# GpSimd takes the sine product of the rotary embedding, VectorE the cosine product out of PSUM

## The reference, cut to what matters

```python
q = l2norm(q) * qs
k = l2norm(k) * ksc
...
q = q * cos * scale + rotate_half(q) * sin * scale
k = k * cos / scale + rotate_half(k) * sin / scale
```

## Time and profile before

| | us |
|---|---|
| median of 3 runs | 1446.84 |
| lowest, highest | 1443.94, 1450.88 |
| the profiled execution | 1459.8 |
| its span, first to last instruction | 1458.1 |

### The profile page before, as it was taken

How to read it: one execution, slowest core, us unless ns; L and a number is a source line. 1 busy time by engine, 2 the same in 40 slices (tenths; PEclk the granted TensorE clock), 3 DMA queues, 4 the chain that set the end, 5 groups by cost and what they waited for, 6 DMA issues and landing times. The chain is left out here.

```text
span 1458.1 us, 23509 instructions
## 1 busy us (share of the span) xinstructions
PE 1124.0 (77%) x8682; PEld 620.1 (43%) x8754; DVE 878.6 (60%) x1738; ACT 768.9 (53%) x1928; POOL 291.5 (20%) x228
## 2 busy tenths in 40 slices
PE   5986788678698668867869877886787976797677
PEld 4752453154374245325437425432534732542353
DVE  5549655963445865596345596468545467648744
ACT  1355674485235556447523556653942453945574
POOL 1105112410101411241010141033202033204210
PEclk9698899889859879988986988997997796999799
DMA  6003101400101310140010131023001014003100
GB/s 260 1 29 117 27 1 58 112 2 15 31 1 45 101 27 1 58 112 2 15 32 1 51 98 23 1 73 98 2 15 32 1 59 111 2 1 123 48 16 15
DMA packets 39201, 66.22 MB, mean 45 GB/s; under 512 B 5408, under 2 KB 19232, under 8 KB 37152
## 3 DMA queue, kind: packets, MB, share of 16 engines
q1 hardware_dynamic: 37920, 62.43, 14.0%
q10 hardware_dynamic: 1152, 2.10, 0.4%
HBM read 13.12 MB, written 2.10 MB: 10 GB/s over the span
## 5 line engine op out<-in xcount | busy, mean ns | idle before, releaser
L494 POOL TENSOR_TENSOR qk<-pc,ps_ 128x512 f32<-128x512 f32 x128 | 194.3, 1518 | 583.8 <-DVE ps_ L1040 583.8
L872 ACT ACTIVATE prob<-bank,negb,inv_norm 128x128 f32<-128x128 f32 x512 | 233.0, 580 | 57.3 <-DVE negb L1087 57.3
L1040 DVE TENSOR_TENSOR ps_<-rot,tab_s 128x512 f32<-128x512 f32 x128 | 172.5, 1347 | 25.9 <-DMA rot<-raw 25.9
L872 ACT ACTIVATION_READ_ACCUMULATOR prob<-bank,negb,inv_norm 128x1 f32 x512 | 163.3, 328 | 0.0
L510 PE MATMUL bank<-hTz,wb_s 128*128 128x512 f32 x256 | 139.5, 675 | 4.3 <-ACT sq L980 4.3
L1085 DVE TENSOR_REDUCE negb<-bank 128x8 f32<-128x1024 f32 x64 | 78.3, 1223 | 94.5 <-PE bank L628 94.4
L976 ACT ACTIVATE raw<-bank,vec_s 128x512 f32<-128x512 f32 x128 | 90.0, 703 | 81.6 <-PE bank L510 46.5
L500 POOL TENSOR_TENSOR prob<-prob,recb 128x512 f32<-128x512 f32 x64 | 66.7, 1041 | 320.1 <-DVE recb L1107 320.1
L1038 DVE TENSOR_TENSOR pc<-raw,tab_s 128x512 f32<-128x512 f32 x128 | 109.3, 854 | 18.2 <-ACT raw L976 18.1
L656 PE MATMUL bank<-probT,vS 128*64 128x64 f32 x1024 | 67.9, 231 | 38.6 <-issue 34.2
L510 PE MATMUL bank<-hTz,w_s 128*128 128x512 f32 (+1 forms) x192 | 87.8, 602 | 12.2 <-DVE hTz L1127 12.2
(11 more groups left out here) (151 smaller groups left out, 2020.8 us busy)
## 6 DMA issues: line engine op xcount, KB each, us to landing
rot<-raw SPq DMA_DIRECT2D x256, 128.0 KB, 2.0
vS<-vB SPq DMA_DIRECT2D x24, 512.0 KB, 4.4
vS<-vB SPq DMA_DIRECT2D x8, 384.0 KB, 5.7
xn_tok<-x SPq DMA_DIRECT2D x5, 512.0 KB, 3.6
tab_s<-tabs SPq DMA_DIRECT2D x1, 2048.0 KB, 21.0
vS<-x SPq DMA_DIRECT2D x4, 512.0 KB, 3.7
out<-vS SPq DMA_DIRECT2D x8, 256.0 KB, 2.4
wb_s<-wb SPq DMA_DIRECT2D x1, 1536.0 KB, 16.6
```

The lines of the kernel that those rows point to most:

```text
L494: pool.tensor_tensor(dst, pc[:, j % 2, :], ps_[:, j % 2, :], ALU.add).then_inc(sum_rdy, 1)
L872: ins = act.activation(prob[:, t % 2, g, h, :], s_bank[t % 2][:, g, h * P:(h + 1) * P], ACT.Exp, bias=negb[:, t % 2, g, h:h + 1], scale=qu ...
L1040: dve.tensor_tensor(ps_[:, j % 2, :], rot[:, jb % 4, :], st, ALU.mult).then_inc(prod_rdy, 1)
```

## The change

Keys: VectorE reads the product in PSUM, times scale vector and cosine, into `pc`, and that frees the bank. GpSimd makes the sine product into `ps_` (`exchanged`) and the sum. Queries: VectorE writes the cosine product back over the bank. GpSimd makes only the sine product, and VectorE adds bank and `ps_` into `qk` (`rotated`), which frees the bank. GpSimd runs one sine product ahead of its sums. ScalarE's square no longer frees the bank but raises `squared`.

With it: `prob` lies over `sq` rather than over `raw` and `rot`; the sums of squares of chunk 1 are handled in two parts, keys (`norms(1)`) and queries (`norms(2)`, within the second tile of the window attention); the shifted values go tile by tile, each with a semaphore of its own, those of chunk 0 behind the exchanges of the key tiles of chunk 1, those of chunk 1 at its end.

```diff
-        v_shifted = sem("values_shifted")
+        v_shifted = [sem(f"values_shifted{t}") for t in range(TILES)]
...
+        squared = sem("squares_ready")
+        turned_rdy = sem("query_cosine_products")
...
+        def key_sums(l, c, k):
+
+            return 4 + (l * CHUNKS + c) * 4 + k
...
-                        if jb % B_QK == B_QK - 1:
-                            c = jb // B_QK % CHUNKS
-                            for t in range(c * TPC, (c + 1) * TPC):
+                        if jb // B_QK % CHUNKS:
+                            k = jb % B_QK
+                            for t in range(TPC, TILES) if k == B_QK - 1 else (k,) if k < TPC else ():
                                 taken(sp, values_use(l, t))
-                            if l:
-                                sp.wait_ge(win_heads, on(l, 0))
-                            t0, t1 = c * TPC, (c + 1) * TPC
-                            sp.dma_start(vS[64:128, t0:t1, :], vB[0:64, t0:t1, :]).then_inc(v_shifted, 16)
-                            u1 = min(t1, TILES - 1)
-                            sp.dma_start(vS[0:64, t0 + 1:u1 + 1, :], vB[64:128, t0:u1, :]).then_inc(v_shifted, 16)
+                                if t == TPC:
+                                    sp.wait_ge(sums_turned, 3 * l + 3)
+                                if l:
+                                    sp.wait_ge(win_heads, on(l, 0))
+                                sp.dma_start(vS[64:128, t, :], vB[0:64, t, :]).then_inc(v_shifted[t], 16)
+                                if t + 1 < TILES:
+                                    sp.dma_start(vS[0:64, t + 1, :], vB[64:128, t, :]).then_inc(v_shifted[t + 1], 16)
...
+                    def exchanged(l, c, k):
+
+                        j = pair(l, c, k)
+                        jb = j - 4
+                        pool.wait_ge(rot_rdy[jb % 4], 32 * (jb // 4 + 1))
+                        if 2 <= k < 6:
+                            pool.wait_ge(sum_rdy, key_sums(l, c, k - 2) + 1)
+                        elif jb >= 2:
+                            l0, c0, k0 = (jb - 2) // 16, (jb - 2) // 8 % 2, (jb - 2) % 8
+                            taken(pool, qk_use(l0, c0, k0))
+                        else:
+                            pool.wait_ge(sum_rdy, 4)
+                        pool.tensor_tensor(ps_[:, j % 2, :], rot[:, jb % 4, :],
+                                           tab_s[:, 3 if k < 4 else 1, cc(c)], ALU.mult).then_inc(prod_rdy, 1)
...
+                                    exchanged(br, 0, 0)
+                                if k + 1 < B_QK or c + 1 < CHUNKS:
+                                    exchanged(br, c + (k + 1) // B_QK, (k + 1) % B_QK)
+                                if k >= 4:
+                                    continue
+                                pool.wait_ge(prod_rdy, j - 4 + 1)
+                                taken(pool, qk_use(br, c, k))
+                                pool.tensor_tensor(qk[:, qk_tile(k), cc(c)], pc[:, j % 2, :], ps_[:, j % 2, :],
                                                    ALU.add).then_inc(sum_rdy, 1)
...
+                        if t % TPC == 0:
+                            for k in range(4):
+                                taken(pe, qk_use(l, t // TPC, 4 + k))
...
-                                taken(pe, qk_use(l, c, k))
-                                mm = pe.matmul(bank[32 * m:32 * m + 32, 4 + c, :], sum_s[:, part, :], sq[:, m, :],
-                                               start=(part == 0), stop=(part == 1), skip_group_check=True)
+                                pe.wait_ge(squared, pair(l, c, k) - 3)
+                                alone = c == 1
+                                mm = pe.matmul(bank[32 * m:32 * m + 32, 4 + (c and not part), :], sum_s[:, part, :],
+                                               sq[:, m, :], start=(alone or part == 0), stop=(alone or part == 1),
+                                               skip_group_check=True)
...
-                                if tt == 0:
+                                if c == 0 and tt == 0:
                                     sum_squares(c, 1)
-                                if tt == 1:
-                                    turn_sums(c)
+                                if c == 0 and tt == 1:
+                                    turn_sums(0)
+                                if c and tt == 0:
+                                    turn_sums(1)
+                                if c and tt == 1:
+                                    sum_squares(c, 1)
+                        turn_sums(2)
...
-                                    act.wait_ge(prod_rdy, jb - 3)
+                                    act.wait_ge(rot_rdy[jb % 4], 32 * (jb // 4))
...
-                                act.activation(sq[:, jb % 4, :], bank[:, i % RING, :], ACT.Square)\
-                                   .then_inc(drained[i % RING], 1)
+                                act.activation(sq[:, jb % 4, :], bank[:, i % RING, :], ACT.Square).then_inc(squared, 1)
...
+                            if c:
+                                copy_sums(1)
...
+                        elif not A and k < 4:
+                            back = (key_sums(br, c, k - 2) if k >= 2 else key_sums(br, c - 1, k + 2) if c else
+                                    key_sums(br - 1, 1, k + 2) if br else 2 + k)
+                            dve.wait_ge(sum_rdy, back + 1)
...
-                            jb = j - 4
-                            dve.wait_ge(raw_rdy, RAW0[br] + c * 8 + k + 1)
-                            dve.tensor_tensor(pc[:, j % 2, :], raw[:, jb % 4, :], ct, ALU.mult)
-                            dve.wait_ge(rot_rdy[jb % 4], 32 * (jb // 4 + 1))
-                            dve.tensor_tensor(ps_[:, j % 2, :], rot[:, jb % 4, :], st, ALU.mult).then_inc(prod_rdy, 1)
+                            qs = V_L + br * VL_N + VL_QS + qk_tile(k) // 4
+                            dve.wait_ge(squared, j - 3)
+                            if k >= 4:
+                                dve.scalar_tensor_tensor(bank[:, i % RING, :], bank[:, i % RING, :], vec_s[:, qs:qs + 1], ct,
+                                                         ALU.mult, ALU.mult).then_inc(turned_rdy, 1)
+                                return
+                            dve.scalar_tensor_tensor(pc[:, j % 2, :], bank[:, i % RING, :], vec_s[:, qs:qs + 1], ct,
+                                                     ALU.mult, ALU.mult).then_inc(drained[i % RING], 1)
+
+                    def rotated(l, c, k):
+
+                        i, jb = qk_use(l, c, k), pair(l, c, k) - 4
+                        dve.wait_ge(turned_rdy, (l * CHUNKS + c) * 4 + k - 3)
+                        dve.wait_ge(prod_rdy, jb + 1)
+                        dve.tensor_tensor(qk[:, qk_tile(k), cc(c)], bank[:, i % RING, :], ps_[:, pair(l, c, k) % 2, :],
+                                          ALU.add).then_inc(drained[i % RING], 1)
...
+                            if t == 1:
+                                norms(2)
...
+                                if k >= 5:
+                                    rotated(l, c, k - 1)
+                            rotated(l, c, B_QK - 1)
...
                         norms(1)
-                        for k in range(4, B_QK):
-                            dve.wait_ge(sum_rdy, pair(l, 1, k) + 1)
                         scale(1, range(4))
-                        window_attention(l)
+                        window_attention(l, norms)
```

More of the change, by code:

```diff
@@ L166, in program @@
             pass
-        with nc.sbuf_tensor("prob", [P, 2, 2, 4, P], F32) as prob, nc.sbuf_tensor("probT", [P, 2, 2, 4, P], F32) as probT:
+        with nc.sbuf_tensor("probT", [P, 2, 2, 4, P], F32) as probT:
             pass
@@ L170, in program @@
         rot = sb("rot", [P, 4, CH])
+        with nc.sbuf_tensor("prob", [P, 2, 2, 4, P], F32) as prob:
+            pass
         sq = sb("sq", [P, 4, CH])
@@ L289, in inv_root @@
             if root is not None:
-                v, t, s = (z.rearrange("p (a e) -> p a e", e=4) for z in (v, t, s))
+                v, t, s = (z.rearrange("p (a e) -> p a e", e=root.shape[-1]) for z in (v, t, s))
                 y = root
@@ L880, in window_lay @@
                         act.wait_ge(win_turned, 2 * on(l, t) + 2)
+                        if t == 0:
+                            act.wait_ge(prod_rdy, (l + 1) * CHUNKS * B_QK)
                         if on(l, t) >= 2:
@@ L962, in _, with copy_sums @@
                     for l in range(LAYERS):
+                        def copy_sums(n):
+                            act.wait_ge(ss_done, l * 4 + n + 2)
+                            act.activation(ss[:, n % 2, :], bank[:, 4 + n % 2, :], ACT.Copy).then_inc(sums_copied, 1)
                         def copy_norms(c):
@@ L1184, in scale @@
                                 i = norm_use(l, c, k)
-                                dve.wait_ge(sum_rdy, pair(l, c, k) + 1)
```

(1 more changed line is left out.)

54 lines of the change are left out of this document (30 added, 24 removed).

## The result

The changed kernel takes 1539.43 us (median of 4 runs, 1537.63 to 1540.57). Before, measured beside it, took 1448.86. The ratio is 1.0613 with a 95% interval of 1.0552 to 1.0675, so 6.1% slower. The forecast was 1503, in a range of 1466 to 1542: slower was right, the size was too small by 36 us. The profiled execution has a span of 1538.5 us (1458.1 before) and a mean granted clock of 0.838 (0.877).

What follows compares the result with a forecast made beforehand. No engine is full; VectorE and GpSimd alternate, waiting for each other over SBUF. Added terms 5.6 + 1 + 0.5 = 7.1 us a pass, 57 for eight: 1517 profiled, 1503 as median, range 1466 to 1542.

Steps and rivals of the forecast that it cites:

- The mechanism: Second chunk's last queries: waits for PSUM banks set the chunk's end, 1503 us in all; chance 0.78.
- Rival 2: Whole pass: exclusion gone, no exchange waits for a bank; 1378 us, weaker form about 1435; chance 0.07 together.
- Rival 3: No change: everything at its low end, +1.2 a pass less what `norms` saves; 1440 to 1454 us; chance 0.05.
- One sign missed: Passes of layer 1, first cosine product to second `norms`, would take 45 to 49 us; under 42 would refute.
- First chunk: Second exchange at 4.1 us, eleven GpSimd instructions at 1.22 each, VectorE's last sum ends at 18.3, before 19.1.
- Between the chunks: Fourth value product waits for VectorE's last sum; product, copy, exchange follow; GpSimd idle 5.5 us (layer 0: until about 28).
- First part of chunk 1: Second chunk to first query's sine product: 8 GpSimd instructions, 9.8 us, plus 1.5 for SP's copies delaying the second exchange.
- Last part: Second chunk's last queries: bank-wait chain 10.8 us at full clock; half level adds 2.9, half taken; pass 5.6 later.
- Behind the pass: Second `norms` to `scale`: cost 0 at TensorE's full level, 3.4 us at the half one; 1 taken.
- Third `norms`: Second attention tile: 11 linked VectorE instructions, 2.4 us in 2.86 idle, GpSimd's product holding the first; 0.5 us stands out.
- The last multiplication: Whole kernel: 7.1 us a pass, 57 for eight, on profiled 1459.8 gives 1517; factor 0.991 to the median gives 1503.
- Rival 4: TensorE at the half level in both places and behind the pass: 15 us a pass, 1567 us; chance 0.10.

Runs made afterwards that it cites:

- the dummies: Changed kernel plus bfloat16 products into unused bank 7 where TensorE waits for a bank: 1503.10 us, ratio 1.0337 to the kernel before.
- the change repaired: Changed kernel with each query sum behind its own cosine product, norm products late, shifted values at the end, third `norms` before attention: 1447.63 us, ratio 0.9961.
- cosine in SBUF repaired: Changed kernel with query cosine product in SBUF, VectorE summing two SBUF tiles, norm products and shifted values late, third `norms` first: 1452.49 us, ratio 0.9976.

## Why the prediction was right or wrong

**The mechanism, right.** Banks released by VectorE's sum behind GpSimd set the end of the second chunk. The waits of the last two query products and the first value product on L1105 show it, and late norm products, which take those waits away, give back 69 of 91 us. The first GpSimd gap, SP's copies and the absence of 1.65 and 1.75 are as described. Rival 2 (the exclusion alone counts) fell: it is gone, and the kernel is slower. Rival 3 fell too. One sign missed: the passes of layer 1 are 49.6 to 51.5 us from the first cosine product, not 45 to 49. The measured time lies only 3 us inside the upper end of the range.

**The steps**, from the first copy of batch 0, layer 1:

| step | forecast | measured |
|---|---|---|
| last sum of the first chunk ends | 19.1 | 19.7 |
| from there to the second chunk's first sine product | 5.5 | 5.9 (7.5 in batches 1 and 3) |
| from there to the end of the first query's | 11.3 | 11.7 |
| from there to `norms` | 12.2 | 13.6 |
| sum | 48.1 | 50.9 |

- **First chunk**: GpSimd works without a break from the first exchange on, so the cosine product's later start costs nothing. Its second product starts 0.3 earlier than forecast (4.66 from the copy), and the eleven instructions from there take 14.2 us and not 13.4. My value of 1.22 was right back to back (three in 3.72), but a product that waits for the sum just ahead of it starts 1.41 after that sum, in 4 of the 11 cases.
- **Between the chunks**: the number came out near, but partly by luck, for the wait was another. The fourth value product doesn't wait for the last sum (done at 272.61). TensorE's only wait here in layer 1 is that of the first value product for the first query's sum. From there it works without a break to the second chunk's first product, 6.6 us later, through value products, sums of squares and their transposition, most of which my chain left out:

```profile
267.58 2.07 PE L543 MATMUL bank<-wb_s,hTz 128*128 128x512 f32 x2 [1.97 <-DVE qk L1105]
...
274.17 3.60 PE L543 MATMUL bank<-hTz,wb_s 128*128 128x512 f32 x8
```

  In batches 1 and 3 more of this work is at the half level, and it takes 8.2 us, which is the other 1.6: the second value product in batch 3, and GpSimd's gap behind it, against the same product in batch 0:

```profile
1404.77 2.08 PE L543 MATMUL bank<-wb_s,hTz 128*128 128x512 f32 x2
```

```profile
1413.47 1.26 POOL L494 TENSOR_TENSOR ps_<-rot,tab_s 128x512 f32<-128x512 f32 x1 [8.34 <-DMA rot<-raw]
```

```profile
271.05 1.12 PE L543 MATMUL bank<-wb_s,hTz 128*128 128x512 f32 x2
```

  In layer 0 the idle time of GpSimd is 11.3 to 11.9, where the forecast of 28 comes to 9.7 + 0.8: 1 us more. The mean products and the sums of squares take 1.9 to 2.05 us each there, the half level too. TensorE's only waits there are for the sums of the first two queries.
- **First part of chunk 1**: SP's copies cost 1.3 for the forecast 1.5. Eight instructions take 10.4 and not 9.8, for the same 1.41 as in the first chunk.
- **Last part, the step that failed**: the two bounds were right and the value between them was wrong. At the full level I had 10.8; the dummies show 11.3. With the half level 10.8 + 2.9 = 13.7; measured 13.6. I took half of the half level. The granted clock is 0.50 from 292 to the end, where every wait for a bank is also a wait of TensorE. Nothing in the earlier trace rows spoke for half of it, though I read them too strictly: the 4 us right behind the idle stretch, 264 to 268, stood at 0.65, and only those from 268 at 0.50.
- **Behind the pass**: forecast +1, measured 0.0. TensorE stood at the half level there before already: the granted clock from the second `norms` to the first maxima was 0.60 to 0.77, and it is 0.77 to 0.79 in the change. The way takes 12.2 in both.
- **Third `norms`**: forecast +0.5. It takes 3.3 us from 321.01 for my 2.4, since its second instruction is held from 0.18 to 1.04, and 2.86 are idle: 0.4 by itself. But the +0.7 of attention has another source, as moving the call gave nothing.
- **The last multiplication**: 10.0 for 7.1 us a layer is 23 of the 36 us missed. The other 13 are my factor of 0.991 from the profiled execution to the median. Before, the profiled one was a long one of its kernel (1459.8 for 1446.8); after, it is 1540 for 1539. Three of its eight attentions took 46.9 to 47.0 us and the others 44.6 to 44.8; that is some 7 of the 13.

**Rival 4** put the half level everywhere at 15 us a layer. Its part for the last stretch came true, its 3.4 behind the pass did not. Half level in the last part alone would have made 8.5 a layer and 1515 us.

**Where the expected gain went.** Taking the exclusion away frees VectorE for nothing as long as the stage is bound by GpSimd plus the gap between the chunks. Three arrangements with all repairs or none come to the same time within 5 us: before (the exclusion, no wait for a bank between the chunks), the change repaired (no exclusion, a gap of 7.1), cosine in SBUF repaired (some of each). In the repaired change a pass of layer 1 is GpSimd's from end to end: 3.4 us to the first exchange, 31.0 for its 24 instructions, 7.1 of gap and 1.0 to `norms`, 42.5 in all. No version can be told to be faster than the kernel before.

**Open**: what sets the steps of attention (44.9, 46.2, 46.9 and 48.2 us), and why the stretch between two batches takes 112.5, 118 or 122 us with the same code. The steps go with a second fall of TensorE's granted clock within attention; no run changes that alone. No run gave the ring a fifth bank either, which would be the direct test of the bank waits.

## What to carry to other kernels

Ask of every operation that is moved who releases the bank it reads. A PSUM bank that is held until the slowest engine's result has been added costs the chain from its release through the next product, copy and transfer, once for each place where the ring runs full; here it cost more than the port conflict. Where TensorE waits for such banks again and again, as in the last part here, price the stretch at the half level and not at a value in between (13.7 us by that price, 13.6 measured). Look also in TensorE's own order for what stands ahead of the product that you think is waiting. And before moving a stall, ask which ring it came from: with as many uses as banks between two tiles, another order only puts it elsewhere.

## What the hardware showed

- A GpSimd instruction over two full tiles starts 1.22 to 1.23 us after the one before it, but 1.41 when it is a product that waits for the sum just ahead of it. No run has such a product without the wait. GpSimd with the four repairs, batch 0, layer 1:

```profile
266.58 1.27 POOL L527 TENSOR_TENSOR qk<-pc,ps_ 128x512 f32<-128x512 f32 x1
267.99 1.27 POOL L494 TENSOR_TENSOR ps_<-rot,tab_s 128x512 f32<-128x512 f32 x1
269.22 1.26 POOL L527 TENSOR_TENSOR qk<-pc,ps_ 128x512 f32<-128x512 f32 x1
```

- VectorE's product out of PSUM and back into the same bank takes 751 ns, as into SBUF (751).
- A small VectorE instruction with one SBUF operand is also held by GpSimd. In the change, behind GpSimd's product that begins at 321.18 and takes 1.04; the same instruction with GpSimd idle, in the kernel with the third `norms` first. It is 1.04 to 1.05 in all eight layers of the one and 0.18 in all of the other:

```profile
321.21 1.04 DVE L297 TENSOR_SCALAR inv_norm<-nw 128x32 int32<-128x32 int32 x1
```

```profile
307.87 0.18 DVE L297 TENSOR_SCALAR inv_norm<-nw 128x32 int32<-128x32 int32 x1
```

The Trainium skill names this case (SBUF — State Buffer, "Who interferes with whom"): a `tensor_scalar` can run in a mode that takes both ports and is then excluded by GpSimd. The trace agrees, by 1.04 against 0.18 us.

- 32 dummy products a layer, whose results nobody reads, made the changed kernel 36 us faster and the clock 0.898 for 0.838. With the four repairs they gave nothing that could be told.
